# A macaron block on one core: key projection in its own bank, smaller first load, later loads held back

## The chip, the cores and the metric

One core of a Trainium2 chip runs the whole program. The metric is the device time of one execution in microseconds, from start to end. The core has TensorE (PE, matrix products into PSUM banks), VectorE (DVE), ScalarE (ACT), GpSimd (POOL), and SyncE (SP), which here only issues transfers. Each engine runs its own list of instructions in order; semaphores tie them together.

## The reference, cut to what matters

The input is 8 sequences of 512 rows with 128 features. Three blocks follow one another: a feed-forward block, an attention-like block inside segments, and the feed-forward block again.

```python
x = x + 0.5 * ffn(layernorm(x))
x = x + attn(layernorm(x))          # per-position scores in segments of 64
x = x + 0.5 * ffn(layernorm(x))

def ffn(x):
    x = conv1d(x, conv_w, width 3) + conv_b
    q, k, v = split(x @ wqkv.T + bqkv)                 # 16 heads of 8
    ctx = softmax(q @ k.T / sqrt(8)) @ v               # 512 x 512 per head
    x = layernorm(x + ctx @ wo.T + bo) * g1 + b1
    probs = softmax(x @ gate_w + gate_b)               # 8 experts, all used
    y = sum_e probs[e] * (relu(x @ w1[e] + b1[e]) @ w2[e] + b2[e])   # 512 wide
    return layernorm(x + y) * g2 + b2
```

Products are made to nearly full precision: an operand is split into a high and a low part, and three passes (high by high, low by high, high by low) are summed.

## The kernel before

The 16 applications of the feed-forward block (8 sequences, twice) are **units**. A unit's work is spread over 256 **ticks**; an iteration is 64 ticks, and in iteration i the kernel works at the same time on unit i+1 (its input, convolution and projections, ticks T = -64 to 0), unit i (scores, T = 0 to 63), unit i-1 (T = 64 to 127) and unit i-2 (T = 128 to 191). The function `walk` goes through the ticks and `tick` holds, for each engine, what is issued at each T, so the order of work on every engine is written out by hand. From iteration 6 on the middle block of one sequence (`mid`) is woven in. Iteration -1 has only unit 0's first part: it is the prologue.

What a unit does, with the names that matter here:
- T = -46: SP loads the unit's input into `f_xn` (for unit 0 at the very start). T = -43 to -40: VectorE makes its statistics and normalises it; T = -38: TensorE transposes it.
- T = -28: the convolution, nine passes into the bank `misc`; ACT evicts it twice, into `ch` (high part, f_ch) and into `conv` (f_c); VectorE makes the low part `cl` (f_cl).
- T = -26 and -23: the query and key projections, three passes each into `misc`; ACT evicts the high part (f_p1), VectorE the low part (f_p2). `misc` is one PSUM bank that some twenty uses of an iteration share; `wait_misc` makes TensorE wait until the use before is read.
- T = -24 and -21: SP stores the parts of query and key to DRAM (`q_parts_dram`, `k_parts_dram`), three transfers each. From there they come back as **packed rows** in `Qp` and `Kp`: rows for the score maxima (use 0, "max") and rows for the probabilities (use 1, "probs"). `LOADS_AT` gives the ticks and `LOAD_CHUNKS` the pairs of heads that each load holds; each load is two transfers (two halves of the heads) of 24 rows.
- T = 0 to 62, every second tick: scores of one tile (a pair of heads and a quarter of the queries; 8 pairs, 32 tiles) for the maxima; VectorE reduces each (`negmax`). After each 8 tiles POOL splits the maxima, TensorE turns them, ACT copies them to `m_rows`, and SP stores these into rows of `Qp` (16 KB, wait `a_m_in`).
- T = 24 to 86: the scores for the probabilities, with the maxima subtracted, then ACT's exponential and the product with V. At T = 24 and for unit 0 this begins together with tile 12 of the maxima.
- T = 112 on: the experts. Their weights are loaded (POOL's queue) and split during iteration 0, one every four ticks.

```python
LOAD_CHUNKS = (((0, 5), (5, PAIRS)), ((0, 4), (4, PAIRS)))
...
LOADS_AT = {-19: (0, 0, 0), -16: (1, 0, 0), -7: (0, 1, 0), -6: (1, 1, 0),
            1: (0, 0, 1), 2: (1, 0, 1), 25: (0, 1, 1), 26: (1, 1, 1)}   # T: (Q or K, use, chunk)
```

SP's list is in order too: an instruction that waits holds all that stand behind it. In the prologue and in iteration 0 SP issues: unit 0's input, weights and vectors, a copy of half of x to `stream_dram`, fills of `Kp` and `Qp`, the parts, the packed rows, the input of unit 1 (T = -46 of unit 1, that is tick 18), the maxima of tiles 0 to 7 (tick 20), further packed rows (ticks 25, 26).

Of the kernel before, what the change touches and what calls it, by code (L numbers as in the profile page):

```python
# [16 lines left out]
TC = S // 128  # L17
# [22 lines left out]
LOAD_CHUNKS = (((0, 5), (5, PAIRS)), ((0, 4), (4, PAIRS)))  # L40
# [11 lines left out]
MID_FIRST = 6  # L52

# [19 lines left out]
def macaron(nc, x, Wq, bq, Wk, bk, Wv, bv, Wo, bo, conv_w, conv_b, wqkv, bqkv, wo, bo2, ln1_g, ln1_b,  # L73
            gate_w, gate_b, w1, b1, w2, b2, ln2_g, ln2_b, out):
    with ExitStack() as ctx:
# [130 lines left out]
        def chunks(tile):  # L206
# [9 lines left out]
        LAST_UNIT = UNITS - 1  # L216
        misc_uses = sorted(
            [(19 + 16 * g - TICKS * b, b, "a_mr", 4, g + 1) for g, b in ((0, 0), (1, 0), (2, 0), (3, 1))]
            + [(60 + 32 * g - TICKS * b, b, "a_norm", 2, g + 1) for g, b in ((0, 0), (1, 1))]
            + [(30, 1, "c_cTs", 1, 1), (34, 1, "c_x1p", 1, 1), (46, 1, "c_x1h", 1, 1), (50, 1, "c_lg", 1, 1),  # L220
               (54, 1, "c_prTs", 1, 1), (55, 2, "e_t", 1, 1)]
            + [(26, -1, "f_xl", 1, 1), (36, -1, "f_cl", 1, 1), (38, -1, "f_p2", 2, 1), (41, -1, "f_p2", 2, 2),
               (57, -1, "f_vs", 1, 1)]
            + [(8, "mid", "m_xl", 1, 1), (11, "mid", "m_mq", 1, 1), (14, "mid", "m_qk", 1, 1),
               (20, "mid", "m_sc", 1, 1), (24, "mid", "m_o", 1, 1), (31, "mid", "m_t", 1, 1)],
# [3 lines left out]
        def in_iteration(i0, back):  # L229
            if back == "mid":  # L230
                return MID_FIRST <= i0 < MID_FIRST + B
            return 0 <= i0 - back <= LAST_UNIT

        def wait_misc(pe, tick, i, i0):

            before = [(t, b, n, per, k, 0) for t, b, n, per, k in misc_uses if t < tick]
            earlier = [(t, b, n, per, k, 1) for t, b, n, per, k in misc_uses]
            for t, b, n, per, k, ago in reversed(earlier + before):
                if in_iteration(i0 - ago, b):
                    u = i - ago - (MID_FIRST if b == "mid" else b)  # L240
                    wait(pe, s[n], per * u + k)
                    return
# [6 lines left out]
        def walk(i, parity, i0, unit_tick, mid_tick=None, first=None):  # L249


            for t in range(TICKS):
                if first and in_iteration(i0, 1):
                    first(t + TICKS, Unit(i - 1, (parity - 1) % 2), t, i, i0)
                if mid_tick and in_iteration(i0, "mid"):
                    mid_tick(t, Unit(i - MID_FIRST, parity), i, i0)
# [33 lines left out]

        def evicted_twice(u, n):

            return alone(u, n) or n % 2 == 0
# [16 lines left out]
        def end_block(eng, u):  # L310
# [4 lines left out]
                .then_inc(s["e_zg"], 1)  # L315
            wait(eng, s["e_zg"], u.count(1, 1))
# [5 lines left out]

        NM_AT = {19 + 16 * g: g for g in range(G)}
        CTX_AT = {60 + 32 * g: g for g in range(G // 2)}
# [8 lines left out]
        def _(sp):  # L333
# [24 lines left out]
            load(stream[B // 2:], x[B // 2:], "ld_x")  # L358

# [12 lines left out]
            def tick(T, u, t, i, i0):  # L372

                for k, at in ((0, 40 - TICKS), (1, 43 - TICKS)):
# [19 lines left out]

                if T - 1 in NM_AT:
# [5 lines left out]
                if T == 119:  # L401
# [3 lines left out]
                for e in range(E):  # L405
                    if T == (120 if e < GATE_RING else EXPERTS_AT + DOWN_LAG + 7 + 8 * (e - GATE_RING)):
# [9 lines left out]
                if T == 18 - TICKS and i0 >= 0:  # L416
# [7 lines left out]
                if T == 180:  # L424
# [5 lines left out]
                if T == 191:  # L430
# [7 lines left out]
            def mid(t, b, i, i0):  # L438
                if t == 0:
# [4 lines left out]
                if t == 20:  # L444
                    wait_sp(s["e_stored"], (i - 2) * 16)
                    sp.dma_start(chunks(resid), rows_of(out, b.n % B)).then_inc(s["m_in2"], 16)
                if t == 33:
# [9 lines left out]
        def _(pool):  # L457
# [46 lines left out]
            def tick(T, u, t, i, i0):  # L504
# [8 lines left out]
                if T == 22 - TICKS:  # L513
# [3 lines left out]
                if T + 2 in NM_AT:  # L517
                    g = NM_AT[T + 2]
# [7 lines left out]
                if T == 100:  # L526
# [17 lines left out]
                if T == 185:  # L544
                    inv_std("e", u.n)
                if T == 186:
# [5 lines left out]
                if T == 187 and i0 <= LAST_UNIT + 1:  # L552
                    end_block(pool, u)

            def mid(t, b, i, i0):
                if t == 3:
                    inv_std("m", b.n)
                if t == 32:
# [8 lines left out]
        def _(act):  # L567
# [10 lines left out]
            def tick(T, u, t, i, i0):  # L578
# [7 lines left out]
                if T == 26 - TICKS:  # L586
                    wait(act, s["f_xT"], u.count(1, 1))
                    wait(act, s["f_conv"], u.count(1, 0))
                    if in_iteration(i0, "mid"):
# [5 lines left out]
                if T == 36 - TICKS:  # L595
# [6 lines left out]
                for k, at, bias in ((0, 38 - TICKS, V_BQ), (1, 41 - TICKS, V_BK)):  # L602
# [15 lines left out]
                if T == 57 - TICKS:  # L618
# [9 lines left out]
                if T - 58 in (0, 32):  # L628
                    g = (T - 58) // 32
# [20 lines left out]
                if T == 94:  # L650
                    wait(act, s["c_cT"], u.count(1, 1))
                    act.activation(ctxT[:], misc[:], ACT.Copy).then_inc(s["c_cTs"], 1)
                if T == 110:
# [4 lines left out]
                if T == 115:  # L658
                    wait(act, s["c_lg2"], u.count(1, 1))
                    act.activation(eg[:], lg2[:], ACT.Exp).then_inc(s["c_eg"], 1)  # L660
                if T == 118:
# [16 lines left out]
                if T == 183:  # L678
# [5 lines left out]
            def mid(t, b, i, i0):  # L684
                if t == 8:
                    wait(act, s["m_xT"], b.count(1, 1))
                    wait(act, s["f_conv"], i + 1)
                    act.activation(mxh, misc[:], ACT.Copy).then_inc(s["m_xh"], 1)
                if t == 11:
                    wait(act, s["m_q"], b.count(1, 1))  # L690
                    wait(act, s["gate_out"], 16 * (i - 1))
                    act.activation(mq[:], misc[:], ACT.Identity, bias=col(V_MBQ)).then_inc(s["m_mq"], 1)
                if t == 21:
# [13 lines left out]
        def _(dve):  # L707
# [65 lines left out]
            def tick(T, u, t, i, i0):  # L773
# [26 lines left out]
                if T == 184:  # L800
                    wait(dve, s["e_t"], u.count(1, 1))
                    moments("e", u.n, lambda c: chunk(zn, c))
                    centre("e", u.n, zn)
                if T == 186:
                    normalise("e", u.n, zn, "e_zn")
                if T == 187 and i0 > LAST_UNIT + 1:
                    end_block(dve, u)
# [12 lines left out]
                if T in CTX_AT:  # L820
                    g = CTX_AT[T]

# [14 lines left out]
                if T == 98:  # L837
# [7 lines left out]
                if T == 99:  # L845
                    wait(dve, s["c_x1p"], u.count(1, 1))
                    moments("c", u.n, lambda c: chunk(x1n, c))
                    centre("c", u.n, x1n)
                if T == 102:
                    normalise("c", u.n, x1n, "c_xn")  # L850
                if T == 110:
# [4 lines left out]
                if T == 111:  # L856
# [3 lines left out]
                if T == 114:  # L860
# [9 lines left out]
                if T == 116:  # L870
# [8 lines left out]
                if T == 21 - TICKS:  # L879
                    wait(dve, s["f_in"], u.count(16, 16))  # L880
                    moments("f", u.n, lambda c: chunk(f_xn, c))
                    centre("f", u.n, f_xn)
                if T == 24 - TICKS:
                    normalise("f", u.n, f_xn, "f_xn")
                if T == 26 - TICKS:
# [5 lines left out]
                if T == 36 - TICKS:  # L891
                    wait(dve, s["f_c"], u.count(1, 1))
# [3 lines left out]
                for k, at, bias in ((0, 38 - TICKS, V_BQ), (1, 41 - TICKS, V_BK)):  # L896
# [15 lines left out]
            def mid(t, b, i, i0):  # L912
                if t == 2:
                    wait(dve, s["m_in"], b.count(16, 16))
                    moments("m", b.n, lambda c: chunk(m_xn, c))
                    centre("m", b.n, m_xn)
                if t == 5:
                    normalise("m", b.n, m_xn, "m_xn")
                if t == 9:
                    wait(dve, s["m_xh"], b.count(1, 1))  # L920
                    dve.tensor_tensor(mxl, misc[:], mxh.bitcast(F32), ALU.subtract).then_inc(s["m_xl"], 1)
                if t == 14:
# [4 lines left out]
                if t == 20:  # L927
# [5 lines left out]
                if t == 22:  # L933
# [8 lines left out]
                if t == 23:  # L942
# [3 lines left out]
                if t == 24:  # L946
# [4 lines left out]
                if t == 31:  # L951
# [10 lines left out]
        def _(pe):  # L962
# [8 lines left out]
            def set_up():  # L971
# [13 lines left out]
                pe.wait_ge(s["set_ql"], 1)  # L985
# [45 lines left out]
            def tick(T, u, t, i, i0):  # L1031
                p = u.parity

                if T == 26 - TICKS:
# [7 lines left out]
                if T == 36 - TICKS:  # L1042
# [6 lines left out]
                for k, at in ((0, 38 - TICKS), (1, 41 - TICKS)):  # L1049
# [4 lines left out]
                if T == 57 - TICKS:  # L1054
# [17 lines left out]
                if T in CTX_AT:  # L1072
                    g = CTX_AT[T]
# [6 lines left out]
                if T == 94:  # L1080
# [5 lines left out]
                if T == 98:  # L1086
# [7 lines left out]
                if T == 114:  # L1094
# [4 lines left out]
                if T == 118:  # L1099
# [5 lines left out]
                if T == 183:  # L1105
# [67 lines left out]
            def mid(t, b, i, i0):  # L1173
                if t == 8:
# [5 lines left out]
                for k, at, done in ((0, 11, "m_q"), (1, 14, "m_k"), (2, 24, "m_v")):  # L1180
                    if t == at:
# [3 lines left out]
                if t == 20:  # L1185
# [4 lines left out]
                if t == 31:  # L1190
# [6 lines left out]
            def first(T, u, t, i, i0):  # L1197

                if T == 110:
                    wait_misc(pe, t, i, i0)  # L1200
                    wait(pe, s["c_xn"], u.count(1, 1))
                    for c in range(TC):
                        last = pe.transpose(chunk(misc, c), chunk(x1n, c), ident[:])
                    last.then_inc(s["c_xnT"], 1)

            run(pe, lambda i, p, i0: walk(i, p, i0, tick, mid, first))
# [21 lines left out]
```

## Time and profile before

| | |
|---|---|
| median of 3 runs | 1699.45 us (1698.41 to 1703.68) |
| profiled execution | 1700.64 us, span 1698.9 us |
| TensorE busy | 1565.9 us, 92% |
| VectorE busy | 1181.0 us, 70% |
| ACT busy | 1152.8 us, 68% |
| POOL busy | 982.7 us, 58% |
| mean granted TensorE clock | 0.972 |
| moved by transfers | 137.52 MB |

The span runs from the first to the last instruction; the execution's own time is 1.7 us longer. A busy share is a mean over stages with different limits, so it says where to look, not what a change is worth.

### The profile page before, as it was taken

To read this page: it belongs to the slowest core of one execution; us is meant where nothing else is said; L and a number is where in the kernel's file an instruction comes from. 1 tells how busy PE (TensorE), PEld (TensorE's weight loads), DVE (VectorE), ACT (ScalarE), POOL (GpSimd) and SP (SyncE) were. 2 spreads that over 40 slices of the span, in tenths; PEclk is the share of its full clock that TensorE was granted. 3 is DMA by queue.
4 is the path that set the end of the run, shared out by engine and by line. 5 is a ranking of instruction groups with operands and counts; after the bars stand their busy time and mean duration, and the time that the engine had idled before them with its cause. 6 is when DMAs were issued, how large, how long until landed. Compare 5 with 4: busy or idle time off the path is not lost. (4 is left out here: it accounts for less than half of the span.)

```text
span 1698.9 us, 26990 instructions
## 1 busy us (share of the span) xinstructions
PE 1565.9 (92%) x8690; PEld 875.8 (52%) x8690; DVE 1181.0 (70%) x1885; ACT 1152.8 (68%) x1684; POOL 982.7 (58%) x925
## 2 busy tenths in 40 slices
PE   4888999999999999999999999999999999999986
PEld 2324555555555455554555545555554555554565
DVE  4766666767767777777677776777777767657475
ACT  2556767777777667676676766767666677776865
POOL 3412657666665657566575755757557566667233
PEclk7679999999999999999999999999999999999998
DMA  7523323241514323252241512425133231511010
GB/s 190 143 65 95 76 68 90 76 95 39 138 45 106 82 77 89 51 135 60 74 102 33 144 51 74 102 53 130 45 102 80 75 96 39 137 39 45 27 44 25
DMA packets 85853, 137.52 MB, mean 81 GB/s; under 512 B 8977, under 2 KB 49602, under 8 KB 81090
## 3 DMA queue, kind: packets, MB, share of 16 engines
q1 hardware_dynamic: 84434, 131.60, 30.2%
q0 software_dynamic: 1280, 4.20, 1.0%
q8 instruction: 72, 1.18, 0.3%
q14 instruction: 67, 0.55, 0.1%
HBM read 102.73 MB, written 32.77 MB: 80 GB/s over the span
## 5 line engine op out<-in xcount | busy, mean ns | idle before, releaser
L535 POOL TENSOR_TENSOR hidl<-hid,hidh 128x512 fp32r<-128x512 f32 x456 | 584.9, 1296 | 507.5 <-DVE hidh L780 321.9
L818 DVE TENSOR_REDUCE negmax<-score 128x2 f32<-128x1024 f32 x484 | 591.0, 1221 | 260.4 <-PE score L1003 257.4
L647 ACT ACTIVATE probs<-score 128x1024 f32<-128x1024 f32 x468 | 480.5, 1027 | 132.7 <-PE score L1023 130.7
L676 ACT ACTIVATE hid<-hid_y,cols 128x512 f32<-128x512 f32 x484 | 332.0, 686 | 180.7 <-PE hid_y L969 141.1
L1140 PE MATMUL ctx_ps<-probs,V 128*18 128x512 f32 x2048 | 276.8, 613 | 0.0
L1003 PE MATMUL score<-Kp,Qp 24*128 24x512 f32 x968 | 245.1, 501 | 29.4 <-DVE negmax L818 16.8
L1023 PE MATMUL score<-Qp,Kp 32*128 32x512 f32 (+1 forms) x1024 | 269.0, 506 | 3.4 <-ACT probs L640 3.3
L965 PE MATMUL hid_y<-x1h,w1h 128*128 128x512 f32 x484 | 232.5, 480 | 17.2 <-ACT hid L676 14.9
L673 ACT ACTIVATE hidh<-hid_y,cols 128x512 fp32r<-128x512 f32 x256 | 175.5, 686 | 76.7 <-PE hid_y L969 72.8
L543 POOL TENSOR_TENSOR yacc<-yacc,gated 128x512 f32<-128x512 f32 x128 | 176.3, 1377 | 65.5 <-DVE gated L796 65.5
L965 PE MATMUL hid_y<-hidh,w2h 128*128 128x512 f32 x512 | 206.5, 403 | 6.1 <-DVE gated L796 6.1
L969 PE MATMUL hid_y<-x1l,w1h 128*128 128x512 f32 x484 | 192.9, 399 | 12.5 <-DVE x1l L858 12.5
L969 PE MATMUL hid_y<-hidl,w2h 128*128 128x512 f32 x512 | 203.2, 397 | 0.0
L966 PE MATMUL hid_y<-hidh,w2l 128*128 128x512 f32 x512 | 201.0, 393 | 0.0
L966 PE MATMUL hid_y<-x1h,w1l 128*128 128x512 f32 x484 | 190.6, 394 | 0.0
L1003 PEld LDWEIGHTS score<-Kp,Qp 24*128 24x128 f32 x968 | 91.1, 184 | 192.1 <-issue 137.0
L965 PEld LDWEIGHTS hid_y<-x1h,w1h 128*128 128x128 f32 x484 | 90.9, 188 | 181.3 <-ACT hid L676 96.8
L965 PEld LDWEIGHTS hid_y<-hidh,w2h 128*128 128x128 f32 x512 | 96.1, 188 | 48.9 <-issue 13.3
L969 PEld LDWEIGHTS hid_y<-x1l,w1h 128*128 128x128 f32 x484 | 90.9, 188 | 40.5 <-DVE x1l L858 19.2
L1023 PEld LDWEIGHTS score<-Qp,Kp 32*128 32x128 f32 (+1 forms) x1024 | 99.6, 184 | 16.9 <-ACT probs L640 8.1
L969 PEld LDWEIGHTS hid_y<-hidl,w2h 128*128 128x128 f32 x512 | 96.2, 188 | 21.9
L966 PEld LDWEIGHTS hid_y<-hidh,w2l 128*128 128x128 f32 x512 | 96.4, 188 | 20.7
(184 smaller groups left out, 1905.8 us busy)
## 6 DMA issues: line engine op xcount, KB each, us to landing
gate_b<-gate_dram SPq DMA_DIRECT2D x128, 256.0 KB, 3.8
q_parts_dram<-q_parts SPq DMA_DIRECT2D x48, 256.0 KB, 3.0
k_parts_dram<-k_parts SPq DMA_DIRECT2D x48, 256.0 KB, 3.0
Qp<-q_parts_dram SPq DMA_DIRECT2D x64, 192.0 KB
Kp<-k_parts_dram SPq DMA_DIRECT2D x64, 192.0 KB
Qp<-q_parts_dram SPq DMA_DIRECT2D x32, 240.0 KB
Kp<-k_parts_dram SPq DMA_DIRECT2D x32, 240.0 KB
Qp<-q_parts_dram SPq DMA_DIRECT2D x32, 144.0 KB
```

Of the source, the lines that this page charges most:

```text
L535: pool.tensor_tensor(hidl[:, n % RING, :], hid[:, n % 2, :], hidh[:, n % RING, :].bitcast(F32), ALU.subtract).then_inc(s["h_lo"], 1)
L543: pool.tensor_tensor(ya[:], ya[:], gated[:], ALU.add).then_inc(s["y_acc"], 1)
L647: act.activation(probs[:, n % 2, 2 * j:2 * j + 2, :], score2[:], ACT.Exp, scale=SCALE)\
L673: act.activation(hidh[:, n % RING, :], hid_bank(u, n)[:], ACT.Relu, bias=col(n))\
L676: act.activation(hid[:, n % 2, :], hid_bank(u, n), ACT.Relu, bias=col(n))\
L818: dve.tensor_reduce(negmax[:, g % 2, :, k % 8], banks_for_max(u.count(32, k))[:], AX.X, ALU.max, negate=True).then_inc(s["a_max"], 1)
L965: pe.matmul(dst, hi, rhi, start=start, stop=False)
L966: pe.matmul(dst, lo, rhi, start=False, stop=False)
L969: return pe.matmul(dst, hi, rlo, start=False, stop=stop)
L1003: last = pe.matmul(banks_for_max(32 * n + k)[:, half, :], Qp[first:end, pair, qc * 128:(qc + 1) * 128], Kp[first:end, pair, :], start=True ...
L1023: last = pe.matmul(score2[:, half, :], Kp[first:end, 2 * g + j, kc * 128:(kc + 1) * 128], Qp[first:end, 2 * g + j, :], start=True, stop=True)
L1140: last = pe.matmul(ctx_ps[32 * j:32 * j + 2 * VC, :], V[p][:, kc, HG * half + 2 * bank + pair, VC * place:VC * place + 2 * VC], probs[:, n ...
```

## The change

The diff has these parts. (1) The first chunk of the rows for the maxima holds pairs 0 to 2 (six heads) and the second pairs 3 to 7, in every unit. (2) For unit 0, all loads of packed rows but the first chunk for the maxima wait for the first scores (`a_s1` at 1). (3) In the prologue the key projection goes to the bank `hid_ps` in place of `misc`. (4) The copy to `stream_dram` moves from SP's opening to tick 28 of unit 0. (5) In the prologue the convolution waits for `set_cl` (low convolution weights), and the projections wait for `set_ql`. (6) In every unit `cl` is made after the first eviction `ch`; the second eviction waits for it, and the bank is free at `f_c`, not `f_cl`. The ticks get names in a table `AT`, with the same values; the turning of x1n is at 109.5, which is the place that it had (before all else of tick 110). `end_block` is cut into two functions called at the same tick.

```diff
-LOAD_CHUNKS = (((0, 5), (5, PAIRS)), ((0, 4), (4, PAIRS)))
+LOAD_CHUNKS = (((0, 3), (3, PAIRS)), ((0, 4), (4, PAIRS)))
...
+AT = {
+    "f_load": -46, "f_stats": -43, "f_centre": -43, "f_rs": -42, "f_norm": -40,
+    "f_xT": -38, "f_xh": -38, "f_xl": -38, "f_conv": -28, "f_ch": -28, "f_cl": -28,
+    "f_q": -26, "f_q1": -26, "f_q2": -26, "f_k": -23, "f_k1": -23, "f_k2": -23, "f_qs": -24, "f_ks": -21,
...
-            + [(26, -1, "f_xl", 1, 1), (36, -1, "f_cl", 1, 1), (38, -1, "f_p2", 2, 1), (41, -1, "f_p2", 2, 2),
-               (57, -1, "f_vs", 1, 1)]
...
+               misc_use("f_conv", "f_c", 1, 1), misc_use("f_q", "f_p2", 2, 1), misc_use("f_k", "f_p2", 2, 2),
+               misc_use("f_v", "f_vs", 1, 1)]
...
+        def bank_of_part(k, i0):
+
+            return hid_ps if k == 1 and i0 < 0 else misc[:]
...
 # SP
-            load(stream[B // 2:], x[B // 2:], "ld_x")
...
                 if T in LOADS_AT:
                     k, use, chunk = LOADS_AT[T]
+                    if u.n == 0 and (use, chunk) != (0, 0):
+                        wait_sp(s["a_s1"], 1)
                     lo, hi = LOAD_CHUNKS[use][chunk]
...
+                if u.n == 0 and T == 28:
+                    load(stream[B // 2:], x[B // 2:], "ld_x")
...
 # ACT
                     act.activation(ch[:], misc[:], ACT.Identity, bias=col(V_CONV)).then_inc(s["f_ch"], 1)
                     wait(act, s["c_x1"], u.n - 1)
+                    wait(act, s["f_cl"], u.count(1, 1))
                     act.activation(conv[u.parity][:], misc[:], ACT.Identity, bias=col(V_CONV))\
                         .then_inc(s["f_c"], 1)
...
-                        act.activation(parts[k][:, 0, :], misc[:], ACT.Identity, bias=col(bias))\
+                        act.activation(parts[k][:, 0, :], bank_of_part(k, i0), ACT.Identity, bias=col(bias))\
...
 # VectorE
-                    wait(dve, s["f_c"], u.count(1, 1))
+                    wait(dve, s["f_ch"], u.count(1, 1))
                     dve.scalar_tensor_tensor(out=cl[:], in0=misc[:], scalar=col(V_CONV),
...
-                        dve.scalar_tensor_tensor(out=parts[k][:, 1, :], in0=misc[:], scalar=col(bias),
+                        dve.scalar_tensor_tensor(out=parts[k][:, 1, :], in0=bank_of_part(k, i0), scalar=col(bias),
...
 # TensorE
-                pe.wait_ge(s["set_ql"], 1)
+                pe.wait_ge(s["set_cl"], 1)
...
-                        wait_misc(pe, t, i, i0)
+                        if k == 0 or i0 >= 0:
+                            wait_misc(pe, t, i, i0)
                         wait(pe, s["f_cl"], u.count(1, 1))
-                        three(misc[:], qkh[:, k, :], qkl[:, k, :], ch[:], cl[:]).then_inc(s["f_qk"], 1)
+                        if i0 < 0:
+                            pe.wait_ge(s["set_ql"], 1)
+                        three(bank_of_part(k, i0), qkh[:, k, :], qkl[:, k, :], ch[:], cl[:]).then_inc(s["f_qk"], 1)
```

## Rows read from the trace of the kernel before

**Rows 1.** The page, its part 2: TensorE's granted clock in tenths, by 40 slices.
```profile
PEclk7679999999999999999999999999999999999998
```
**Rows 2.** The timeline, 9 to 24 us: start, duration, what, [idle before and releaser].
```profile
11.26 0.80 PE L965 MATMUL misc<-xh,cwh 128*128 128x512 f32 x1 [0.46 <-DVE wvT L721]
...
11.64 0.64 SPq L335 DMA_DIRECT2D stream_dram<-in_L_attn_x  x1
...
14.57 0.40 PE L969 MATMUL misc<-xl,cwh 128*128 128x512 f32 x1
...
17.26 0.47 PE L965 MATMUL misc<-ch,qkh 128*128 128x512 f32 x1 [2.29 <-DVE cl L893]
...
19.37 1.92 SPq L382 DMA_DIRECT2D q_parts_dram<-q_parts  x3
...
20.11 0.79 PE L965 MATMUL misc<-ch,qkh 128*128 128x512 f32 x1 [1.56 <-DVE q_parts L899]
...
21.80 0.69 ACT L606 ACTIVATE k_parts<-misc,cols 128x512 fp32r<-128x512 f32 x1 [2.52 <-PE misc L969]
...
22.58 1.82 SPq L382 DMA_DIRECT2D k_parts_dram<-k_parts  x3
```
**Rows 3.** The timeline, 27 to 64 us.
```profile
27.35 0.70 SPq L390 DMA_DIRECT2D Kp<-k_parts_dram  x2
...
31.77 0.41 SPq L419 DMA_DIRECT2D f_xn<-in_L_attn_x  x1
...
34.84 0.79 PE L1003 MATMUL score<-Kp,Qp 24*128 24x512 f32 x2 [9.02 <-DMA Kp<-k_parts_dram]
...
35.67 1.23 DVE L818 TENSOR_REDUCE negmax<-score 128x2 f32<-128x1024 f32 x1 [9.46 <-PE score L1003]
...
46.63 0.74 SPq L398 DMA_DIRECT2D Qp<-m_rows  x1
...
48.14 0.86 DVE L750 BATCH_NORM_STATS2 f_st<-f_xn 128x6 f32<-128x128 f32 x4
...
48.81 0.79 PE L1003 MATMUL score<-Kp,Qp 24*128 24x512 f32 x2 [0.88 <-DMA Qp<-m_rows]
...
51.44 0.79 PE L1003 MATMUL hid_y<-Kp,Qp 24*128 24x512 f32 x2 [1.83 <-DVE negmax L818]
...
63.78 0.71 SPq L398 DMA_DIRECT2D Qp<-m_rows  x1
```
**Rows 4.** Transfers by issue, three short stretches (issued near 32, 34.8, 11.6): KB, us to landing.
```profile
f_xn<-in_L_attn_x SPq DMA_DIRECT2D x1, 256.0 KB, 16.2
...
gate_b<-in_L_ffn_w POOLq DMA_DIRECT2D x1, 256.0 KB, 12.2
...
stream_dram<-in_L_attn_x SPq DMA_DIRECT2D x1, 6.0
```
**Rows 5.** The timeline around the convolution of an ordinary unit, 418 to 424 us.
```profile
420.16 0.69 ACT L598 ACTIVATE ch<-misc,cols 128x512 fp32r<-128x512 f32 x1 [1.17 <-PE misc L969]
...
420.75 0.68 ACT L600 ACTIVATE conv<-misc,cols 128x512 f32<-128x512 f32 x1
...
421.46 0.75 DVE L893 SCALAR_TENSOR_TENSOR cl<-misc,cols,ch 128x512 fp32r<-128x512 f32 x1 [0.83 <-ACT conv L600]
...
422.05 0.69 ACT L676 ACTIVATE hid<-hid_y,cols 128x512 f32<-128x512 f32 x1 [0.62 <-PE hid_y L969]
...
423.07 0.50 PE L965 MATMUL misc<-ch,qkh 128*128 128x512 f32 x1
...
423.27 1.03 ACT L647 ACTIVATE probs<-score 128x1024 f32<-128x1024 f32 x1 [0.53 <-PE score L1023]
```
**Rows 6.** Line 893 (VectorE makes cl): what it waited for, who waited: us, times.
```profile
  ACT conv L600: 18.6, 16
...
  PE misc L965: 3.8, 3
```
**Rows 7.** Windows: busy us of PE, PEld, DVE, ACT, POOL; PEclk, DMA share, GB/s.
```profile
60.00:70.00 10.00, 9.83 (x39) 4.27 (x31) 2.75 (x4) 4.42 (x9) 4.03 (x6) 0.56 0.19 54
```

More of the change, by code:

```diff
@@ L229, in in_iteration @@
         def in_iteration(i0, back):
-            if back == "mid":
-                return MID_FIRST <= i0 < MID_FIRST + B
+            if isinstance(back, tuple):
+                return MID_FIRST <= i0 - back[1] < MID_FIRST + B
             return 0 <= i0 - back <= LAST_UNIT
@@ L247, in run, with walk @@
                 iteration(i, i % 2, i)
[L249 to L256, printed above, removed]
+        def walk(i, parity, i0, unit_tick, mid_tick=None):
+            for t in (h / 2 if h % 2 else h // 2 for h in range(2 * TICKS)):
+                for back in (0, -1):
+                    if mid_tick and in_iteration(i0, ("mid", back)):
+                        mid_tick(t + TICKS * back, Unit(i - back - MID_FIRST, parity), t, i, i0)
                 for back in (2, 1, 0, -1):
@@ L372, in tick @@
             def tick(T, u, t, i, i0):
-                for k, at in ((0, 40 - TICKS), (1, 43 - TICKS)):
+                for k, at in ((0, AT["f_qs"]), (1, AT["f_ks"])):
                     if T == at:
@@ L414, in tick @@
                             .then_inc(s["gate_in"][e % GATE_RING], 16)
-                if T == 18 - TICKS and i0 >= 0:
+                if T == AT["f_load"] and i0 >= 0:
                     wait_sp(s["f_xT"], u.count(1, 0))
@@ L551, in tick, with mid @@
                                        ALU.add).then_inc(s["e_zb"], 1)
[L552 to L556, printed above, removed]
+                if T == AT["e_zg"] and i0 <= LAST_UNIT + 1:
+                    scale_out(pool, u)
+                if T == AT["e_x"] and i0 <= LAST_UNIT + 1:
+                    add_out(pool, u)
+            def mid(T, b, t, i, i0):
+                if T == AT["m_rs"]:
                     inv_std("m", b.n)
-                if t == 32:
+                if T == AT["m_x"]:
                     wait(pool, s["m_t"], b.count(1, 1))
@@ L599, in tick @@
                     wait(act, s["c_x1"], u.n - 1)
+                    wait(act, s["f_cl"], u.count(1, 1))
                     act.activation(conv[u.parity][:], misc[:], ACT.Identity, bias=col(V_CONV))\
                         .then_inc(s["f_c"], 1)
[L602 removed]
+                for k, at, bias in ((0, AT["f_q1"], V_BQ), (1, AT["f_k1"], V_BK)):
                     if T == at:
@@ L1093, in tick @@
                     last.then_inc(s["c_x1"], 1)
-                if T == 114:
+                if T == AT["xnT"]:
+                    wait_misc(pe, t, i, i0)
+                    wait(pe, s["c_xn"], u.count(1, 1))
+                    for c in range(TC):
+                        last = pe.transpose(chunk(misc, c), chunk(x1n, c), ident[:])
+                    last.then_inc(s["c_xnT"], 1)
+                if T == AT["gate"]:
                     wait_misc(pe, t, i, i0)
@@ L1179, in mid @@
                     last.then_inc(s["m_xT"], 1)
-                for k, at, done in ((0, 11, "m_q"), (1, 14, "m_k"), (2, 24, "m_v")):
-                    if t == at:
+                for k, at, done in ((0, AT["m_q"], "m_q"), (1, AT["m_k"], "m_k"), (2, AT["m_v"], "m_v")):
+                    if T == at:
                         wait_misc(pe, t, i, i0)
@@ L1195, in mid @@
                     last.then_inc(s["m_out"], 1)
[L1197 to L1206, printed above, removed]
+            run(pe, lambda i, p, i0: walk(i, p, i0, tick, mid))
 _INS = ["L0_attn_x", "L0_attn_Wq", "L0_attn_bq", "L0_attn_Wk", "L0_attn_bk", "L0_attn_Wv", "L0_attn_bv",
```

190 lines of the change are left out of this document (107 added, 83 removed).

## The prediction

> **What bounds the kernel now.** I read the page first: TensorE is busy 92% of the span, as the table above has it, and its granted clock is 0.6 to 0.7 in most of the early slices and 0.9 and more afterwards [rows 1]. From the second unit on, nothing in the change takes work off TensorE, so a gain has to come from the start, where TensorE is idle, or from a wait it has later. So I read the timeline of the first 60 us next. There the reader is to see a single chain: convolution, query projection, its two evictions, key projection, its evictions, three stores of the key parts to DRAM, the load of the packed key rows, and at 34.84 the first scores, which had waited for that load [rows 2, 3]. From 35.67 to 48.14 VectorE reduces eleven score tiles, one every 1.13 us. (I count the tiles of a unit from 0; tile 0 is that at 34.84.) Then comes the place that decides this case: at 46.63 the small load of the row maxima is issued, TensorE's tile 12 stands until 48.81 for it, VectorE starts the statistics of the second unit's input at 48.14, and tile 13, at 51.44, waits for the VectorE queue behind those statistics [rows 3]. The third view, transfers by issue, says why 48: the input of unit 1, issued at 31.77 as the last of SP's loads, took 16.2 us, so it landed at 48.0, and a weight load of the POOL queue took 12.2 us where the copy of the stream, alone, had taken 6.0 [rows 4]. From the start of the key load to 48 the transfers are a backlog. Last, the timeline around an ordinary unit's convolution, since one edit touches all units [rows 5].
>
> **The change part by part.** All times are made against the profiled execution (span 1698.9, its own time 1700.64; the median of the three runs is 1699.45, 1.2 less, so differences are added to the median).
>
> *TensorE's setup waits for the low convolution weights only.* The first convolution pass had waited 0.46 us for the copy of wvT [rows 2]; the wait that stays ends before that. Gain at most 0.46. The passes quicken during the convolution (0.80 us the first, 0.40 the last [rows 2]), so part of it is lost; I take 0.35.
>
> *The low part is made before the second eviction.* Before, ACT evicts twice, then VectorE makes cl. After: ACT, VectorE, ACT, and the query projection needs the bank free (second eviction) too. Three steps in series both times (0.69, 0.68, 0.75 in [rows 5]), one more hand-over and one lost overlap of two ACT instructions (0.59 apart though 0.69 long), 0.15 us. In the prologue this leaves 0.2 to 0.3 of the above at the query projection: 17.26 becomes 17.0. In an ordinary unit: ch ends 420.85, cl would run 420.9 to 421.65, the second eviction 421.7 to 422.4, so ACT's next eviction moves from 422.05 to about 422.3, and ends at 423.0. The query projection starts at 423.07 anyway, behind other work of TensorE, and ACT's next exponential waited for scores until 423.27 [rows 5]. What hides it is TensorE's 2 us of expert and score passes; without that cover it costs 0.3 to 0.9 a unit. Cover is missing in units 1 and 2, which have no experts beside them (those of unit 0 begin at its tick 112): TensorE waited for cl in three units, 3.8 us in total [rows 6], of which 2.29 at 17.26 in the prologue [rows 2] leave 1.5 for those two, and ACT's exponentials stand behind the moved eviction, 0.1 to 0.6 each. Together +0.5 (0.2 to 1.2).
>
> *Keys in their own bank.* The key projection started at 20.11 because the bank was being read; now it follows the query's third pass (about 18.3). Its first eviction moves from 21.80 to 19.5. But SP issues in order: the query's three stores took 1.92 us from 19.37 [rows 2], now from about 19.05 to 21.0, and only then the key's. So the key's stores start at 21.0, not 22.58: gain 1.6, not 2.3.
>
> *First load of six heads.* 24 rows of five pairs of 2 KB were 240 KB for each of two halves; now 144 KB. The key load was issued at 27.35 and let TensorE go at 34.84, 7.5 us [rows 3], partly behind the query's 480 KB. From 27.35 to 48.0 there passed, by the issues, 480 (key) + 768 (rows for the probabilities) + 576 (second chunk) + 256 (input) KB of SP and four weight loads of 256 KB: 3104 KB in 20.6 us, 151 KB/us. A small transfer takes at most 2.2 us (46.63 to 48.81). So the new key load: issue 25.6, 0.35 for its second half, 2.2, 288 KB at 151 = 1.9: first scores at 30.0 (28.5 to 31), 4.8 us earlier.
>
> *The other loads wait for the first scores, and SP with them.* Queued behind that wait on SP are the rows for the probabilities (768 KB), the second chunk, grown from 576 to 960 KB, then the input of unit 1 (256), then the row maxima. They used to be issued right behind the key's load, the input by 31.77 [rows 3]; now from 30.0 + 0.8 = 30.9. The bytes ahead of the input are then 768 + 960 + 256 = 1984 KB, and three or four weight loads (the first deferred one now runs in the gap, but an eighth comes early): 2752 to 3008 KB, at 151 KB/us 18.3 to 19.9 us. The input lands at 49.2 to 50.8; I take 50.1. Before: 48.0. The second chunk, needed at tile 12 and no longer at tile 20, lands just ahead of it at 48 to 49. Tile 12 would be wanted at about 44 (48.81 less 4.8). So the 4.8 us won at tile 0 are waited away before tile 12, since what ends last there is now the transfers: row maxima behind the input, then VectorE's statistics, 2.1 us, then tile 13. Net +2.1 (+0.5 to +3.7 with a rate of 165 or 140 KB/us).
> The Trainium skill ("DMA: Bandwidth & Descriptors", section "Queues, rings and completion order") says that each engine takes the descriptors of one queue in ring order; by that too the small load of row maxima can't pass the large ones. The trace agrees, with TensorE released for it at 48.81, after the input's 48.0.
>
> *The copy of the stream moves* from 11.64 [rows 2] to tick 28 of unit 0. It had landed 6.0 us after its issue [rows 4], at 17.6, before the first store at 19.37: moving it wins nothing on the chain. Its new place is behind the last packed rows (768 KB, 5 us after the input), so about 55 to 62; the next small load it could hold was issued at 63.78 [rows 3], some 2 us later in the new kernel. Cover 3 us; if gone, 1 to 3 us. From the second unit on the smaller first chunk and larger second are issued 23 ticks or more before use: nothing.
>
> Sum: 2.1 + 0.5 = +2.6, so **1702 us**, +0.15%. From about 54 on TensorE is busy nearly without a break (9.83 of 10 us [rows 7]), so the delay carries to the end.
>
> **The rivals.**
> *A, the gain is kept*: the deferred loads run faster than 151 KB/us because the weight loads got through in the gap. To keep all, the input must land by 43.3, that is 1984 KB and two or three weight loads in 12.4 us, 200 to 220 KB/us. Time: 1699.45 - 4.8 + 0.5 = 1695. Against it: the 16.2 and 12.2 us landings. A half-way case (input at 46) gives 1698.
> The Trainium skill has a fit ("DMA: Bandwidth & Descriptors", section "Anatomy of one DMA — SWDGE (gpsimd) path"): 2.0 us and the bytes over 436 GB/s. By it the old key load would take 3.1 us; the trace shows 7.5 (behind other loads), so the trace doesn't bear it out here. By it the deferred loads are in by about 38 to 41, the outcome is A, 1695.
> *B, ACT's wait for cl shows in every unit*: the ordinary unit's cover is only 0.3 us at the exponential. Place: tick 36 of each of 15 units; price 0.35 to 0.9 each, +5 to +14, time 1705 to 1713. It decides once ACT's release after the second eviction comes over 0.3 us later than I put it. For: VectorE waited for ACT there 16 times of 16, 18.6 us in total [rows 6]. Against: TensorE waited for cl in three units only [rows 6].
> *C, the clock moves*: from 60 to 70 it was 0.56 [rows 7], and the page's first slices of 42 us stand at 0.7, 0.6, 0.7 and 0.9 [rows 1]: in the start the clock changes between its levels more than once. A changed idle pattern (six us more idle at 44 to 50) may shift a stretch of 3 us or so between the two levels (1.2 and 2.4 GHz), worth half of it, -3 to +3.
> *D, the change does nothing*: weights split earlier win back what the input loses, 1699.5.
>
> **Chances and range.** Forecast 0.50 (its own range 1699.8 to 1704.5), A with its half-way case 0.18, B 0.14, C as what decides 0.10, D 0.08. What a measurement of this kernel can tell from no change is 0.3%, 5.1 us: below 1694.3 or above 1704.6. Faster: a third of A and a little of C, 0.08. Slower: all of B, the upper end of the forecast and of C, 0.20. Same: 0.72. Range 1695 to 1707: below lie the lower part of A, above half of B.
>
> **What would show it.** In the new profile: key stores issued at 21.0; first scores at 30.0; tile 11 at about 43 and tile 12 not before 50; the landing of unit 1's input over 15 us after an issue at 34; the statistics at 50.1; tile 13 at 53.5. An ordinary unit is as long as before. Wrong if the input lands before 48, if TensorE waits for the packed rows beyond the input, or if units 3 to 15 take longer.

## The result and the profile after

The changed kernel takes 1708.53 us (median of 22 runs, 1701.39 to 1715.42), the kernel before 1700.9 (22 runs, 1695.65 to 1712.55): ratio 1.0041, 95% interval 1.0027 to 1.0054. The forecast was 1702 with a range up to 1707. By my bound of 0.3% it is slower. Every ratio in this text is against runs of the kernel before that were made beside the kernel in question; the medians of those were 1698.9 to 1700.9, so medians of different experiments are not compared with one another.

The profiled execution was the quickest of the 22: 1701.39, span 1699.7. It is a bad stand-in for the median, and the first thing to note is how the runs differ from one another: with a mean granted TensorE clock of 0.972 the time was 1701.39, with 0.966 to 0.967 it was 1705.6 to 1711.3, with 0.963 it was 1713 and more. Over the 22 runs clock and time are correlated at -0.95. So a second profiled execution of the same kernel was taken (after_again, below), with 1708.7 us and clock 0.967.

First the start, in the timeline of the changed kernel (start, duration, what, [idle before, releaser]); it answers to [rows 2, 3].

```profile
15.79 0.50 PE L1007 MATMUL misc<-ch,qkh 128*128 128x512 f32 x1 [2.34 <-ACT conv L636]
...
19.87 1.82 SPq L411 DMA_DIRECT2D k_parts_dram<-k_parts  x3
...
25.36 0.70 SPq L421 DMA_DIRECT2D Kp<-k_parts_dram  x2
...
30.65 0.80 PE L1045 MATMUL score<-Kp,Qp 24*128 24x512 f32 x2 [10.25 <-DMA Kp<-k_parts_dram]
...
31.68 0.70 SPq L421 DMA_DIRECT2D Qp<-q_parts_dram  x2
...
35.33 0.41 SPq L452 DMA_DIRECT2D f_xn<-in_L_attn_x  x1
...
42.44 0.72 SPq L431 DMA_DIRECT2D Qp<-m_rows  x1
...
47.41 0.87 DVE L786 BATCH_NORM_STATS2 f_st<-f_xn 128x6 f32<-128x128 f32 x4 [3.38 <-DMA f_xn<-in_L_attn_x]
...
47.94 0.79 PE L1045 MATMUL score<-Kp,Qp 24*128 24x512 f32 x2 [4.20 <-DMA Qp<-m_rows]
...
50.73 0.79 PE L1045 MATMUL hid_y<-Kp,Qp 24*128 24x512 f32 x2 [2.00 <-DVE negmax L857]
```

The reader is to see 4.2 us won at the first scores (30.65 for 34.84) and given back in one wait: tile 12 stands 4.20 us for the row maxima, issued at 42.44 and released at 47.94, in a queue behind the held-back loads. VectorE, too, now waits 3.38 us, for unit 1's input. Tile 13 is 0.7 us ahead, 50.73 for 51.44.

Then a place that the prediction did not look at: tile 4 of unit 1, where the row maxima of unit 0's last eight tiles are wanted. The kernel before, timeline:

```profile
97.31 0.70 SPq L390 DMA_DIRECT2D Qp<-q_parts_dram  x2
98.19 0.70 SPq L390 DMA_DIRECT2D Kp<-k_parts_dram  x2
101.85 0.68 SPq L398 DMA_DIRECT2D Qp<-m_rows  x1
...
103.96 0.51 PE L1003 MATMUL score<-Kp,Qp 24*128 24x512 f32 x2 [0.38 <-DMA Qp<-m_rows]
```

and the changed kernel, timeline:

```profile
94.61 0.70 SPq L421 DMA_DIRECT2D Qp<-q_parts_dram  x2
95.49 0.70 SPq L421 DMA_DIRECT2D Kp<-k_parts_dram  x2
99.15 0.68 SPq L431 DMA_DIRECT2D Qp<-m_rows  x1
...
103.28 0.50 PE L1045 MATMUL score<-Kp,Qp 24*128 24x512 f32 x2 [2.40 <-DMA Qp<-m_rows]
```

Both issue the last loads of the second chunk of unit 1's rows for the maxima 3.7 us ahead of the row maxima (ticks 1 and 2, tick 4). Before, that chunk was 576 KB and the maxima let TensorE go 2.1 us after their issue; now it is 960 KB, and it takes 4.1 us. TensorE stands 2.40 us instead of 0.38. In the whole trace of the kernel before TensorE waits for row maxima in four places (0.88 us at 48.81, 1.47 at 88.61, 0.38 at 103.96, 0.34 at 119.72), in that of the changed kernel in two (4.20 at 47.94, 2.40 at 103.28); from unit 2 on there is no such wait in either.

The windows from 90 to 135 us show what came with it (busy us of PE, PEld, DVE, ACT, POOL, then the granted clock, DMA share, GB/s). The kernel before:

```profile
90.00:135.00 45.00, 39.06 (x207) 14.76 (x200) 28.79 (x38) 25.67 (x51) 4.41 (x10) 0.78 0.20 47
```

The changed kernel:

```profile
90.00:135.00 45.00, 38.05 (x185) 12.53 (x184) 28.51 (x37) 25.05 (x49) 4.20 (x9) 0.69 0.22 46
```

Fewer matmuls are done (185 for 207) in nearly as much busy time (38.05 for 39.06 us), at a mean clock of 0.69 for 0.78 of full speed (2.4 GHz; the lower level is 1.2).

### The profile page after: what moved, and what is told of

The parts are those of the page before. It is cut to its first block and busy times, and to the rows that moved or that the text cites. A ratio compares the mean times of both kernels' runs of the same rounds, so it can differ in the third digit from the quotient of the medians.

```text
span 1699.7 us, 26997 instructions
## 1 busy us (share of the span) xinstructions
PE 1564.2 (92%) x8690; PEld 874.3 (51%) x8690; DVE 1186.9 (70%) x1885; ACT 1153.1 (68%) x1684; POOL 982.7 (58%) x925
```

## The experiments

A short way to read every trace is the start of VectorE's reduction of a given tile, taken from the timeline: it is a sign of TensorE's progress. Tile n of a unit belongs to its tick 2n. The table has all kernels; the last column is how long unit 1 took from tile 2 to tile 16.

| kernel | unit 0 tile 0 | unit 0 tile 12 | unit 1 tile 2 | unit 1 tile 16 | unit 5 tile 0 | tile 2 to 16 |
|---|---|---|---|---|---|---|
| before | 35.67 | 51.30 | 101.58 | 132.26 | 462.72 | 30.7 |
| before_2 | 35.94 | 51.56 | 101.77 | 129.51 | 459.99 | 27.7 |
| after | 31.48 | 50.59 | 98.88 | 133.27 | 464.01 | 34.4 |
| after_again | 31.86 | 52.09 | 101.74 | 136.38 | 469.61 | 34.6 |
| no_six | 31.72 | 52.17 | 100.11 | 133.25 | 470.77 | 33.1 |
| no_defer | 31.44 | 48.94 | 99.12 | 133.30 | 464.03 | 34.2 |
| only_chunk | 33.30 | 52.66 | 100.89 | 135.32 | 466.02 | 34.4 |
| only_six | 36.64 | 52.27 | 101.40 | 132.19 | 465.34 | 30.8 |
| chunk_back | 36.35 | 51.98 | 101.64 | 132.34 | 462.96 | 30.7 |
| late_chunk | 32.43 | 54.08 | 100.64 | 131.73 | 462.54 | 31.1 |
| first_only | 32.02 | 51.45 | 104.29 | 139.84 | 478.87 | 35.6 |
| first_only_2 | 31.85 | 53.18 | 104.20 | 135.32 | 465.90 | 31.1 |
| early_in | 33.18 | 49.58 | 100.67 | 128.40 | 461.49 | 27.7 |
| small_probs | 31.64 | 47.27 | 95.78 | 126.47 | 457.10 | 30.7 |

Five traces have three and five pairs in every unit with the larger chunk at ticks 1 and 2 (after, after_again, no_six, no_defer, only_chunk): 33.1 to 34.6 us. Of the nine others eight have 27.7 to 31.1; the ninth is the first trace of first_only, whose clock was at the low level from 74 to 146 us.

**after_again**: the changed kernel, unchanged.

> The changed kernel itself, unchanged, for a second trace and for the clock of each run. Clock theory: the profiled execution shown so far (span 1699.7, mean granted clock 0.972) was the quickest of 22, while the median is 1708.5; a usual run then has 15 to 20 us more at the low level of the TensorE clock, mean clock 0.966 or so, all of it before 150 us, and the units after that keep their length of 95.7 us. ACT theory (second eviction waits for cl in every unit): the units 3 to 15 are longer by 0.3 us or more each. Time 1706 to 1710 either way.

1708.33 us (12 runs), ratio 1.0049 (1.0033 to 1.0064), span of the trace 1707.0, clock 0.967. As the clock theory said, most of the difference to the first trace is early: tile 12 of unit 0 is at 52.09 for 50.59, the wait at tile 4 of unit 1 is 2.7 us, at the start of unit 2 this trace is 5.6 us behind the first one, and from unit 2 to unit 5 nothing is added. The theory put all of it there; the span is 7.3 us longer, and the rest comes from unit 7 on, in steps of under 1 us. The ACT theory, which wanted 0.3 us or more in each of the units 3 to 15, is out: in the changed kernel's timeline cl starts 95.73 us apart from one unit to the next, in the kernel before 95.69 (325.77 and 421.46).

```profile
326.44 0.75 DVE L934 SCALAR_TENSOR_TENSOR cl<-misc,cols,ch 128x512 fp32r<-128x512 f32 x1 [0.25 <-ACT ch L633]
...
422.17 0.75 DVE L934 SCALAR_TENSOR_TENSOR cl<-misc,cols,ch 128x512 fp32r<-128x512 f32 x1 [0.26 <-ACT ch L633]
423.01 0.69 ACT L636 ACTIVATE conv<-misc,cols 128x512 f32<-128x512 f32 x1 [0.88 <-DVE cl L934]
423.60 0.68 ACT L712 ACTIVATE hid<-hid_y,cols 128x512 f32<-128x512 f32 x1
...
424.36 0.50 PE L1007 MATMUL misc<-ch,qkh 128*128 128x512 f32 x1
```

ACT's eviction of the hidden tile follows the moved one 0.26 us later than before (2.15 us after ch starts for 1.89), and the query projection starts 2.91 us after ch starts in both [rows 5]: the cover held.

**no_six** and **only_six**: part 6 undone in the changed kernel, and part 6 alone in the kernel before.

```diff
-                    wait(act, s["f_cl"], u.count(1, 1))
...
-                    wait(dve, s["f_ch"], u.count(1, 1))
+                    wait(dve, s["f_c"], u.count(1, 1))
```

> The changed kernel with part 6 undone (both evictions before cl, bank free at f_cl); all else as changed. ACT theory: back to the kernel before or below, 1696 to 1701. Clock theory: part 6 matters only through units 1 and 2; 1704 to 1709, mean clock under 0.970.

1708.7 us (8 runs), ratio 1.0057 (1.0034 to 1.008).

> The kernel before with part 6 alone. ACT theory: 1705 or more. Clock theory: within 2 us of the kernel before, 1699 to 1703.

1701.22 us (12 runs), ratio 1.0009 (0.9991 to 1.0026). The order of the evictions is not the cause, from both sides. only_six also has the changed kernel's table of ticks and its new `walk`, so these are not the cause either. That it costs the 0.5 us which I put down for units 1 and 2 can't be told at this precision.

**no_defer**: the wait for the first scores taken out.

```diff
-                    if u.n == 0 and (use, chunk) != (0, 0):
-                        wait_sp(s["a_s1"], 1)
```

> The changed kernel without the wait of unit 0's later loads for the first scores (part 2 undone). TensorE then loses its stall of 4 us before tile 12 since the loads are in the queue earlier; the first scores come at 30.7 to 32. Clock theory with the stall as the cause: 1697 to 1702. If the stall is not the cause: 1706 to 1710.

1706.42 us (12 runs), ratio 1.0049 (1.003 to 1.0068). The stall before tile 12 did not go, as I had expected, but shrank from 4.20 to 2.29 us. Tile 12 of unit 0 is 1.7 us earlier than in the changed kernel (48.94 for 50.59), yet at unit 1's tile 16 both are at 133.3, and the ratio is the changed kernel's. So the stall before tile 12 does not decide, and the first scores came as early (31.44) without holding the loads back. All kernels so far that lose have the wait at unit 1's tile 4: 2.2 to 2.7 us by their lists of waits, against 0.4 in before and only_six. That gave the queue theory, which names part 1: the row maxima now stand behind a chunk of 960 KB, and TensorE waits for them. The clock-only theory, its rival, is that an earlier start moves the low stretches and the sizes don't matter.

**only_chunk** and **chunk_back**: part 1 alone in the kernel before, and part 1 undone in the changed kernel.

```diff
-LOAD_CHUNKS = (((0, 5), (5, PAIRS)), ((0, 4), (4, PAIRS)))
+LOAD_CHUNKS = (((0, 3), (3, PAIRS)), ((0, 4), (4, PAIRS)))
```

> The kernel before with part 1 alone: first chunk of the rows for the maxima three pairs, second five, in every unit. Queue theory: at tick 4 of unit 1 the row maxima now stand behind 960 KB of packed rows instead of 576, so TensorE waits 2 to 3 us there for them (0.4 in the kernel before), with little won at the first scores; offset against the kernel before at least +2 after unit 1's tile 4, and the clock may then stay low to about 130 us: 1702 to 1707. Clock-only theory (the earlier start shifts the low stretches, chunk sizes do not matter): 1698 to 1701 and no wait of 2 us.

1705.25 us (10 runs), ratio 1.0033 (1.0018 to 1.0048). One line makes most or all of the slowdown (the intervals of the two kernels overlap). The trace is of the quickest of the ten runs. Its timeline has the same wait:

```profile
96.62 0.70 SPq L390 DMA_DIRECT2D Qp<-q_parts_dram  x2
97.50 0.70 SPq L390 DMA_DIRECT2D Kp<-k_parts_dram  x2
101.16 0.68 SPq L398 DMA_DIRECT2D Qp<-m_rows  x1
...
105.34 0.49 PE L1003 MATMUL score<-Kp,Qp 24*128 24x512 f32 x2 [2.44 <-DMA Qp<-m_rows]
```

and its windows the same clock:

```profile
90.00:135.00 45.00, 38.01 (x183) 13.64 (x179) 26.97 (x36) 23.61 (x47) 3.80 (x7) 0.67 0.25 53
```

> The changed kernel with part 1 undone (five and three pairs), all else kept. Queue theory: first scores about 32 to 33, tile 12 at 47 to 48, the wait for the row maxima at unit 1's tile 4 back to under 0.6 us: 1697 to 1701. Clock-only theory: the loss between 90 and 132 us stays, 1705 to 1710.

1700.95 us (10 runs), ratio 1.0012 (0.9995 to 1.0029). The wait is 0.37 us and the clock 0.78. The expectation for the start was wrong: the first scores were at 35.5, not 32 to 33, with 480 KB for the query and for the key, so in this trace the separate bank won nothing that reached the first scores. The traces say what did: from the issue of the key load to the first scores it took 7.5 to 8.7 us with 480 KB (before 7.5, only_six 7.5, before_2 7.7, chunk_back 8.7) and 4.2 to 5.7 us with 288 KB (only_chunk 4.2, after_again 4.3, after 5.3, early_in 5.7). So at the first scores the smaller chunk is worth about 3 us. The bank and the weights show at the issue of the key load: 27.35 to 28.27 in the four traces without them, 25.18 to 26.91 in the ten with them. chunk_back is at 26.86 and its load is the slowest of all, which took the 0.5 us back.

**late_chunk**: the test of the cause. Sizes and bytes are as in the changed kernel, but in units 1 to 15 the larger chunk goes behind the row maxima.

```diff
-                if T in LOADS_AT:
-                    k, use, chunk = LOADS_AT[T]
+                moved = {5: 1, 6: 2} if u.n else {}
+                if (T in LOADS_AT and not (u.n and T in (1, 2))) or T in moved:
+                    k, use, chunk = LOADS_AT[moved.get(T, T)]
```

> The changed kernel, but in units 1 to 15 the second chunk of the rows for the maxima (five pairs) is issued at ticks 5 and 6, behind the row maxima of tick 4, not at ticks 1 and 2. Sizes and bytes are as in the changed kernel. Queue theory: the wait for the row maxima at tile 4 of unit 1 falls from 2.4 us to under 0.6, and the time to 1700 to 1704. If the size of the chunk hurts in another way, or the early start does: 1706 to 1710.

1699.95 us (11 runs), ratio 1.0007 (0.9996 to 1.0017). The timeline of unit 1's start:

```profile
100.92 0.68 SPq L432 DMA_DIRECT2D Qp<-m_rows  x1
101.79 0.71 SPq L422 DMA_DIRECT2D Qp<-q_parts_dram  x2
102.69 0.70 SPq L422 DMA_DIRECT2D Kp<-k_parts_dram  x2
103.05 0.49 PE L1046 MATMUL score<-Kp,Qp 24*128 24x512 f32 x2 [0.40 <-DMA Qp<-m_rows]
```

and its window:

```profile
90.00:135.00 45.00, 39.68 (x212) 14.96 (x212) 29.14 (x38) 26.10 (x52) 5.49 (x10) 0.77 0.28 62
```

Every other part of the change is in, the start has the same stall (even longer, 5.01 us), and the slowdown is gone with the wait, from 1.0041 (1.0027 to 1.0054) to 1.0007. What is shown is the cause: a small transfer issued behind a larger load. No run issues the row maxima from another engine's queue, so it is open how much of the wait is the order within SP's queue and how much the sharing of the transfer engines with the larger load.

**first_only** (twice), **early_in**, **small_probs**: can the early start be kept? In first_only three and five pairs are for unit 0 alone; early_in, whose probability rows keep the split after four pairs, also loads unit 1's input before the held-back loads; small_probs also splits unit 0's rows for the probabilities after two pairs. The lines below are small_probs against the changed kernel.

```diff
+def load_chunks(use, n):
+    if n == 0:
+        return (((0, 3), (3, PAIRS)), ((0, 2), (2, PAIRS)))[use]
+    return (((0, 5), (5, PAIRS)), ((0, 4), (4, PAIRS)))[use]
...
+                    if u.n == 0 and T == -7:
+                        wait_sp(s["f_xT"], 1)
+                        sp.dma_start(chunks(f_xn), rows_of(x, 1)).then_inc(s["f_in"], 16)
...
-                if T == AT["f_load"] and i0 >= 0:
+                if T == AT["f_load"] and i0 >= 1:
```

> The changed kernel with three and five pairs in unit 0 alone, five and three in all others. Queue theory: the start of the changed kernel (first scores at 30.7, tile 13 at 50 to 51.5) and no wait at unit 1's tile 4: 1696 to 1701. Clock-only theory: 1705 to 1710.

1705.21 us (12 runs, one of which took 4044.87 us and is not in the ratio), ratio 1.0025 (1.0001 to 1.005); expected were 1696 to 1701. Its trace is the one with the low clock from 74 to 146.

> first_only once more, for a second trace: its first one had the clock at the low level from 74 to 146 us. Theory that an early start followed by the wait before tile 12 brings more low clock, run by run: median 1702 to 1706, clock 0.968 to 0.971, low stretches between 74 and 170 us that differ from the first trace's. If the first trace was a stray: 1699 to 1702.

1702.53 us (10 runs), ratio 1.0021 (1.0005 to 1.0036), clock of the trace 0.970; its low stretches are shorter and lie at 80 to 98 and 114 to 134. The wait at tile 4 is gone (0.4 us in the second trace), yet it is not as quick as late_chunk. Both traces are at 104.2 or 104.3 at unit 1's tile 2, 2.7 us behind the kernel before. In the second trace part of it can be seen, and it is the same mechanism one group of row maxima earlier, at tile 28 of unit 0. The kernel before:

```profile
88.61 0.80 PE L1003 MATMUL score<-Kp,Qp 24*128 24x512 f32 x2 [1.47 <-DMA Qp<-m_rows]
```

first_only_2:

```profile
82.50 0.70 SPq L426 DMA_DIRECT2D Kp<-k_parts_dram  x2
83.94 0.70 SPq L436 DMA_DIRECT2D Qp<-m_rows  x1
...
89.54 0.79 PE L1050 MATMUL score<-Kp,Qp 24*128 24x512 f32 x2 [2.42 <-DMA Qp<-m_rows]
```

With five pairs in unit 1's first chunk 480 KB of keys are issued shortly ahead of these row maxima, here by 1.4 us, and TensorE waits 2.42 us. With three pairs it is 288 KB; in the traces of after, after_again, only_chunk and no_defer there is no wait here, in late_chunk 0.22 us, in no_six 0.86. So part 1 also removes a wait, of 0.9 to 1.5 us in the traces of before and before_2, and late_chunk keeps that. From 90 to 104 us the clock of first_only_2 is 0.66, that of the kernel before 0.90. In the first trace of first_only there is no wait at this tile, only the low clock.

> As first_only, and the input of unit 1 is loaded before the loads that wait for the first scores. The queue in front of the row maxima is 256 KB shorter and VectorE's statistics are not late: tile 12 at 45.5 to 46.5, tile 13 at 47 to 48.5, 2 us before first_only. If what follows passes this on: 1694 to 1699; if the clock takes it back, as first_only.

1697.54 us (10 runs), ratio 0.9992 (0.9972 to 1.0012), which is within the expected 1694 to 1699 and can't be told from the kernel before. Tile 12 was expected at 46 and came at 48.75: moving the input forward only changes the order of the bytes, the row maxima are last as before. VectorE's statistics were early (45.64).

> As early_in, and in unit 0 the rows for the probabilities are split after two pairs instead of four, the rest going at tick 25. The bytes ahead of the row maxima fall by 384 KB. Queue theory: tile 12 at 46 to 46.8 (48.75 in early_in), tile 13 1.5 to 2 us earlier, time 1693 to 1697. If the clock takes the gain back: as early_in, 1697.

1699.94 us (12 runs), ratio 0.9998 (0.9982 to 1.0014); expected were 1693 to 1697. The start, timeline:

```profile
42.60 0.72 SPq L441 DMA_DIRECT2D Qp<-m_rows  x1
...
44.10 0.86 DVE L796 BATCH_NORM_STATS2 f_st<-f_xn 128x6 f32<-128x128 f32 x4
...
44.76 0.80 PE L1055 MATMUL score<-Kp,Qp 24*128 24x512 f32 x2 [0.86 <-DMA Qp<-m_rows]
```

With 384 KB less ahead of the row maxima the wait fell from 3.32 (early_in) to 0.86 us and tile 12 came at 44.76, earlier than expected: the backlog is what held it. Of the 4.0 us between the two traces at tile 12, 1.5 were there at the first scores already (30.81 for 32.35). In this trace the kernel is 5.6 us ahead of the kernel before at unit 5 (457.10 for 462.72); at the last tiles of unit 15 only 1.5 (1566.27 for 1567.76). The rest went in units 8, 10 and 11, up to 3.4 us at a time. Such single losses of 0.3 to 3.4 us are in other traces too, in units 6 to 13, at different units each time. Whether small_probs has them more often is open. No version is shown to be quicker than the kernel before.

**before_2**: the kernel before once more.

> The kernel before once more, for a second trace: span 1695 to 1703, the wait for the row maxima at unit 1's tile 4 near 0.4 us, the low stretches of the clock at other places than in the first trace.

1697.75 us, span 1696.0. The wait is 0.4 us, and the window 90 to 135 has a clock of 0.85. The same program is 2.7 us ahead of its first trace at unit 5, and all of that arises between unit 1's tiles 2 and 16, in the stretch where the clocks differ (0.85 for 0.78).

## Why the prediction was wrong

**The step that failed** is the last sentence of the part on the stream's copy: "From the second unit on the smaller first chunk and larger second are issued 23 ticks or more before use: nothing." The use that I had in mind was that of the chunk. What the larger chunk delays is another transfer that is queued behind it: the row maxima of the previous unit, issued at tick 4, two ticks after the chunk's last load, and wanted at tick 8. The count of ticks was off too, though no wait came of it: keys of the second chunk are issued at tick 2 and used at tick 24, 22 ticks later, and those of the first chunk at tick -16 for tick 0. I had named just this mechanism for unit 0's tile 12 and did not carry it to unit 1's tile 4. A term that I had put at nothing measured 2.0 us of waiting (0.38 to 2.40). Undone by late_chunk, it is worth the difference between the ratios 1.0041 and 1.0007; part 1 alone in the old kernel has 1.0033.

**A second step failed without deciding the score**: "so the delay carries to the end". The delay or lead at tile 12 of unit 0 did not last even to unit 1. late_chunk was 2.8 us late at tile 12 (54.08 for 51.30) and 0.9 us ahead at unit 1's tile 2 (100.64 for 101.58), with a clock of 0.89 for 0.66 between 74 and 90 us; no_defer's lead of 1.7 us over the changed kernel was gone there as well (99.12 for 98.88). A TensorE that is busy 9.83 of 10 us can be at either level of its clock (0.56 in that very window [rows 7]), and the forecast of +2.1 us from tile 13 had no term for that in its sum.

**Why only unit 1, and why more than 2 us.** From unit 2 on TensorE has the experts beside the scores, no wait for row maxima is left, and nothing is added up to unit 5: the changed kernel is 1.1 us behind the kernel before at the start of unit 2 and 1.3 at that of unit 5. In unit 1 the stretch from tile 2 to tile 16 is 3.7 us longer (34.4 for 30.7) though the wait is 2.0 us longer, and the window's clock is 0.65 to 0.69 in the five traces with the wait and 0.75 to 0.86 in the others but the two of first_only (0.50 and 0.67). Of the 7 us by which the median is longer (0.41%) the first trace shows little, since it is of the quickest run; after_again has a further low stretch before unit 2, which costs 2.5 us between tiles 24 and 26 of unit 1. That the wait brings the clock down is argued from these traces and from late_chunk's recovery; no run holds the clock and changes the wait. Rival C (the clock moves) was right in kind, but I gave it as chance of either sign with 3 us, not as what may multiply a wait.

**The start, point by point.** The separate weights wait: first convolution pass 10.61 for 11.26, and in the first trace the passes quickened from the third on, so the query projection was at 15.79, 1.2 us earlier than my 17.0. That quickening was luck of this trace: in after_again, the same program, the passes stayed at 0.63 us up to the last and the projection was at 17.15, as forecast. Key stores at 19.87 and 21.30, forecast 21.0; the key load at 25.36 and 26.74, forecast 25.6, since it waits for the landing of the stores. First scores 30.65 and 31.03, forecast 30.0 (28.5 to 31): right. Held-back loads from 31.68 on, and tile 12 waits until their backlog is through: right as mechanism. Its size: the input landed 12.1 us after 35.33, so at 47.4; by the same count of bytes (2752 to 3008 KB from 31.68) that is 175 to 191 KB/us, not 151. But in after_again it landed at 49.0 and in late_chunk, which has the same start, at 50.9, against a forecast of 50.1: over the three traces the rate was 151 to 191 KB/us, and the forecast is the slow end of what the kernel does. The forecast was +2.1 net at tile 13; measured there were -0.7 (after), +0.8 (after_again) and +2.8 (late_chunk).

The Trainium skill's ring order ("DMA: Bandwidth & Descriptors", section "Queues, rings and completion order"), by which each engine takes the descriptors of one queue in the order of its ring, agrees with this trace: the row maxima issued at 42.44 let TensorE go at 47.94, after the input, issued ahead of them at 35.33, had landed at 47.4. The fit that the prediction took from the same page, for its rival A, is stated there for transfers issued by GpSimd, while the packed rows are issued by SP; neither the old key load (7.5 us for 3.1 by the fit) nor the held-back loads came near it.

**The order of the evictions**: nothing in ordinary units, as forecast; rival B did not happen. In unit 1 the projection waited 0.65 us as before, now for ACT:

```profile
68.13 0.50 PE L1007 MATMUL misc<-ch,qkh 128*128 128x512 f32 x1 [0.65 <-ACT conv L636]
```

**Rival A** came half true for the transfers in one trace (47.4) and in no trace for the time. **Rival D**, no change, is what chunk_back shows without part 1 (1.0012, 0.9995 to 1.0029).

## What to carry to other kernels

When a load grows or moves, list what is issued behind it on the same queue in the next few microseconds, in every stage and not only where the load itself is used: the small transfer that is wanted soon pays. A win at the first instruction of a pipeline is worth only what the next shared resource, here one queue of transfers, can pass on; count the bytes ahead of the next hard wait. And where the runs of one kernel spread by 15 us, take a second trace before reading a cause into the first.

## What the runs showed of the hardware that was not expected

The low clock at the start is nearly free here. The trace of only_chunk (and that of only_six) kept the high level from 18 to 60 us, through 6 us of idle TensorE and more; windows of only_chunk:

```profile
18.00:60.00 42.00, 21.60 (x73) 9.50 (x73) 24.23 (x34) 11.94 (x24) 17.64 (x20) 1.00 0.71 165
```

and of the kernel before:

```profile
18.00:60.00 42.00, 22.25 (x77) 9.61 (x79) 25.18 (x34) 12.87 (x26) 18.09 (x21) 0.50 0.74 172
```

At twice the clock TensorE did no more in this stretch (73 matmuls for 77), since VectorE's reductions and the transfers set its pace; the mean clock of such a run (0.983) says nothing good about its time (span 1699.3). Among the 94 ordinary runs of the kernel before that were made beside the experiments, 27 had a mean clock of 0.979 or more: their median is 1699.6 us, that of the other 67 is 1699.2. In this kernel the mean clock of a run is a sign of its time only as far as the low stretches fall where TensorE sets the pace.
